# Attention bodies with the MLP as one block, maxima eight steps ahead, normalisations in halves, and the scores of a step in two pairs of heads

## The reference, cut to what matters

```
# stage 0: cross attention with a mask per batch, then MLP    (layer 0)
# stage 1: cross attention, no mask                            (layer 1)
# stage 2: self attention with one mask for all, then MLP      (layer 1)
# stage 3: causal self attention                               (layer 2)
# stage 4: cross attention, no mask, then MLP                  (layer 2)
# tail:    RMS norm, cross attention with 64-column heads      (layer 3)
q, k, v = split(norm(x) @ Wq), split(c @ Wk), split(c @ Wv)
s = einsum('bhqd,bhkd->bhqk', q, k) * scale ;  s = where(mask, -inf, s)
x = x + softmax(s) @ v @ Wo + bo
x = x + gelu(norm(x) @ W1 + b1) @ W2 + b2          # W1: 256x1024, W2: 1024x256
```

## Time and profile before

| | |
|---|---|
| median of 3 runs | 5727.45 us (5720.6 to 5732.76) |
| the profiled execution's own time | 5747.48 us |
| its span in the profile | 5745.7 us |
| PE busy | 4965.1 us (86%) |
| DVE busy | 2681.2 us (47%) |
| ACT busy | 2679.4 us (47%) |
| POOL busy | 919.7 us (16%) |
| mean granted PE clock | 0.94 of full speed |

### The profile page before, as it was taken

The page is one execution under the profiler, slowest core; times in us unless marked ns, Lnnn a source line. Parts: engine busy times, 40 slices in busy tenths (PEclk is TensorE's granted clock), DMA queues, the critical chain, the costliest instruction groups (busy, mean ns, idle before and its releaser), DMA issues.

```text
span 5745.7 us, 70587 instructions
## 1 busy us (share of the span) xinstructions
PE 4965.1 (86%) x25988; PEld 2091.8 (36%) x25988; DVE 2681.2 (47%) x5328; ACT 2679.4 (47%) x3337; POOL 919.7 (16%) x831
## 2 busy tenths in 40 slices
PE   6888888878888888888888888888876799999999
PEld 2333333332222343333443343334433333333333
DVE  4444444445556544444334446444441345555444
ACT  3555555454554554454443344565554233333333
POOL 0000010100011000011011111110010233333333
PEclk8999999988999999999998899899998899999999
DMA  1011111011111000101011111100010100000000
GB/s 52 32 34 41 47 37 41 33 53 57 52 48 54 32 29 27 37 34 37 29 50 48 53 63 58 36 32 30 32 47 23 48 12 1 11 12 12 12 12 8
DMA packets 152313, 201.93 MB, mean 35 GB/s; under 512 B 18993, under 2 KB 102321, under 8 KB 150706
## 3 DMA queue, kind: packets, MB, share of 16 engines
q1 hardware_dynamic: 151986, 197.31, 10.1%
HBM read 128.86 MB, written 68.42 MB: 34 GB/s over the span
## 4 chain that ended last, share of the span: by engine, by line
PE 65%; DVE 13%; issue 9%; ACT 6%; DMA 4%; POOL 1%; SPq 1%; DVEq 0%; POOLq 0%; ACTq 0%
PE small L555 12%; PE psT L598 7%; PE small L548 7%; PE psO L616 6%; PE small L665 6%; PE psT L767 4%; DVE nmb L986 4%; PE psS L576 4%; PE psT L602 3%; PE psT L548 2%; PE psT L732 2%; PE psO L782 2%; PE psT L555 2%; PE psT L782 2%; DVE out L983 2%
## 5 line engine op out<-in xcount | busy, mean ns | idle before, releaser
L824 ACT ACTIVATE probs<-psT 128x1024 f32<-128x1024 f32 (+3 forms) x1280 | 1158.7, 958 | 1402.9 <-PE psT L602 632.5
L986 DVE TENSOR_REDUCE nmb<-psS 128x2 bf16<-128x1024 f32 (+3 forms) x768 | 840.4, 1094 | 838.0 <-PE psS L576 535.3
L598 PE MATMUL psT<-low 32*128 32x512 f32 (+3 forms) x5120 | 781.7, 666 | 107.5 <-DVE low L1010 43.8
L983 DVE CUSTOM_DVE_ANT_0 out<-psS,pens_sb 128x512 f32<-128x512 f32 x1024 | 665.8, 688 | 135.8 <-issue 106.9
L616 PE MATMUL psO<-probs,V 128*32 128x512 f32 (+3 forms) x5120 | 684.0, 608 | 0.0
L576 PE MATMUL psS<-out 32*128 32x512 bf16 (+3 forms) x2560 | 501.6, 388 | 207.4 <-DVE nmb L986 132.0
L1128 DVE TENSOR_REDUCE parts<-psS 128x2 bf16<-128x1024 f32 x256 | 314.9, 1230 | 523.7 <-PE psS L754 523.7
L665 PE MATMUL small<-out,W 128*128 128x256 f32 x1536 | 399.6, 405 | 132.3 <-ACT out L859 38.0
L930 ACT ACTIVATE probs<-psT 128x1024 f32<-128x1024 f32 x256 | 262.0, 1023 | 526.1 <-PE psT L770 526.1
L576 PEld LDWEIGHTS psS<-out 32*128 32x128 bf16 x2560 | 123.7, 93 | 814.1 <-DVE nmb L986 326.2
L555 PE MATMUL small<-W,gel 128*128 128x256 f32 x1536 | 357.2, 386 | 16.4 <-DVE low L1010 13.5
(11 more groups left out here) (152 smaller groups left out, 5600.9 us busy)
## 6 DMA issues: line engine op xcount, KB each, us to landing
o_mid<-oT SPq DMA_DIRECT2D x160, 256.0 KB, 2.0
oN<-o_mid SPq DMA_DIRECT2D x160, 128.0 KB
oN<-r_mid SPq DMA_DIRECT2D x80, 256.0 KB
x_mid<-xe SPq DMA_DIRECT2D x40, 512.0 KB, 3.0
xw<-x_mid SPq DMA_DIRECT2D x36, 512.0 KB, 4.6
xe<-x_mid SPq DMA_DIRECT2D x36, 512.0 KB, 4.6
cT<-ctxT SPq DMA_DIRECT2D x20, 512.0 KB, 4.7
W<-wm SPq DMA_DIRECT2D x6, 1024.0 KB, 7.7
```

Of the source, the lines that this page charges most:

```text
L598: last = nc.tensor.matmul(psT[j][:, q0:S], Kf[rows_of(j), q, a, c, kt * P:(kt + 1) * P], Qf[rows_of(j), q, a, c, q0:S], start=True, stop=p ...
L824: nc.scalar.activation(probs[:, i % 2, two, q0:S], psT_all[:, two, q0:S], ACT.Exp, scale=float(DH) ** -0.5)\
L983: nc.vector.tensor_tensor_reduce(junk[:, k, :], psS[k], pens[:, 0, qt * S:(qt + 1) * S], 1.0, -3.0e38, ALU.add, ALU.max, nmb4[:, g % 2, qt ...
L986: nc.vector.tensor_reduce(nmb4[:, g % 2, qt, row:row + 33:32], psS_both[:, :, 0:n], AX, ALU.max)\
```

## The change

- LEAD is 8 in place of 6. The maxima of `cur`'s steps 8 to 15 are computed in steps 0 to 7 of its own body.
- MLP bodies: after step 9 there is one block. PE runs the 8 hidden tiles (two matmul pairs of 128x512 each) into psT banks 0 and 1 in turn, ACT takes each with one gelu of 512 columns, then PE runs the second layer in 8 parts into banks 2 and 3, DVE adds them to xe with two instructions. Between these 16 pieces PE issues the 16 max_scores of `nxt`. In the block PE also issues outputs(9). No exponential is computed in it. The eight f and four z fills are gone from `small`. In the steps 8 to 15 of an MLP body there are no max_scores.
- Other bodies: the maxima of `nxt` run in steps 8 to 15.
- PE's order of a step: max_scores 0; the scores of heads 0 and 1 with their mask, then those of heads 2 and 3 with theirs, each pair with its own wait for the exponential that frees its two banks and its own signal to ACT; even fills; max_scores 1; outputs. Where the odd slot has fills, outputs come ahead of max_scores 1, and the fills behind. The two max_scores of a step swap their pairs of heads.
- Moments and normalisations on DVE are cut in halves of two token tiles in slots of their own, and the slots of all fills are new. In a slot of DVE this work now comes ahead of the readers of fills.
- On ACT the readers of fills come ahead of the copy to oT. On POOL `scale` comes ahead of the second rsqrt of stage 0. On SP the store of group 1's oT comes ahead of the store of x, and an MLP body's x is stored when the block's sums are added.
- gel is 512 columns wide; oT, masks, cw and cn live in other buffers' space.

```diff
-LEAD = 6
+LEAD = 8
-CUR_USES = {True: {"m1": 6, "m2": 14, "m3": 20}, False: {"m1": 7, "m2": 15, "m3": 22}}
-Y_USES = {True: {"y0": 7, "y1": 8}, False: {"y0": 14, "y1": 16}}
-MLP_USES = {"h0": 11, "h1": 12, "fa0": 13, "fa1": 15, "fa2": 17, "fa3": 19, "za0": 21, "za1": 22,
-            "fb0": 23, "fb1": 25, "fb2": 26, "fb3": 27, "zb0": 29, "zb1": 30}
-CTX_USES = {True: {"c0": 8, "c1": 9}, False: {"c0": 11, "c1": 12}}
-NXT_USES = {True: {"x0": 4, "x1": 5, "q0": 9, "k0": 10, "q1": 16, "k1": 18, "v0": 24, "m0": 28, "v1": 31},
-            False: {"x0": 6, "x1": 8, "q0": 10, "k0": 12, "q1": 18, "k1": 20, "v0": 24, "v1": 26, "m0": 29}}
+MLP_AFTER = 9
+CUR_USES = {True: {"m1": 1, "m2": 15, "m3": 17}, False: {"m1": 1, "m2": 15, "m3": 21}}
+Y_USES = {True: {"y0": 10, "y1": 12}, False: {"y0": 17, "y1": 19}}
+MLP_USES = {"h0": 18, "h1": 19}
+CTX_USES = {True: {"c0": 13, "c1": 14}, False: {"c0": 12, "c1": 12}}
+NXT_USES = {True: {"x0": 7, "x1": 8, "q0": 9, "k0": 16, "q1": 21, "k1": 23, "v0": 25, "m0": 27, "v1": 29},
+            False: {"x0": 7, "x1": 9, "q0": 11, "k0": 13, "q1": 23, "m0": 25, "k1": 27, "v0": 29, "v1": 31}}
+MASKS_AT = 15
+X_STATS, X_NORMALISE = (2, 3), (5, 6)
+C_STATS, C_NORMALISE = {True: (8, 9), False: (7, 8)}, {True: (11, 12), False: (10, 11)}
+MLP_STATS, MLP_NORMALISE = (13, 14), (16, 17)
+RECIP_AT = 5
...
             def max_scores(place, u, i, k, ahead):
...
+                for e in range(2):
+                    j = 2 * (1 - k) + e
+                    last = nc.tensor.matmul(psS[e][:, 0:n], Qb[rows_of(j), q, a, c, qt * P:(qt + 1) * P], Kb[rows_of(j), q, c, 0:n],
                                             start=True, stop=u.s != CAUSAL)
...
             def exp_scores(place, u, i):
...
-                if positive(k := count("exp_done", u, 2 * i)):
-                    pe.wait_ge(sem["exp_done"], k)
-                plain = u.s not in (*MASKED, CAUSAL)
-                for j in range(4):
-                    last = nc.tensor.matmul(psT[j][:, q0:S], Kf[rows_of(j), ...], Qf[rows_of(j), ...], start=True, stop=plain)
-                for j in range(4):
-                    if u.s in MASKED: ...
-                last.then_inc(sem["st_full"], 1)
+                for pair in range(2):
+                    if positive(k := count("exp_done", u, 2 * i - 1 + pair)):
+                        pe.wait_ge(sem["exp_done"], k)
+                    for j in (2 * pair, 2 * pair + 1):
+                        last = nc.tensor.matmul(psT[j][:, q0:S], Kf[rows_of(j), ...], Qf[rows_of(j), ...], ...)
+                    for j in (2 * pair, 2 * pair + 1):
+                        if u.s in MASKED: ...
+                        if u.s == CAUSAL: ...
+                    last.then_inc(sem["st_full"], 1)
...
+            def hidden(u, m):
+                if m >= 2:
+                    pe.wait_ge(sem["f_read"], count("f_read", u, m - 1))
+                for c in range(C):
+                    last = nc.tensor.matmul(psT[m % 2], W1[:, c, m * P:(m + 1) * P], hM[:, c, :], start=c == 0, stop=c == C - 1)
+                last.then_inc(sem["f_full"], 1)
+            def from_hidden(u, t, part):
+                if t == 0 and part == 0:
+                    pe.wait_ge(sem["f_read"], count("f_read", u, FC))
+                for m in range(FC // 2 * part, FC // 2 * (part + 1)):
+                    last = nc.tensor.matmul(psT[2 + t // 2][:, (t % 2) * D:(t % 2 + 1) * D], gel[:, m, t * P:(t + 1) * P], W2[:, m, :], ...)
+                if t % 2 and part:
+                    last.then_inc(sem["z_full"], 1)
+            def mlp(place, u, cur, nxt):
+                pe.wait_ge(small_read, place.fills("prev", "h1") + 2)
+                if cur is not None:
+                    pe.wait_ge(sem["exp_done"], count("exp_done", cur, 2 * (MLP_AFTER + 1)))
+                for m in range(FC):
+                    hidden(u, m)
+                    maximum_next(m)
+                if cur is not None:
+                    outputs(cur, MLP_AFTER)
+                for t in range(T):
+                    for part in range(2):
+                        from_hidden(u, t, part)
+                        maximum_next(FC + 2 * t + part)
...
+                    if maxima:
+                        max_scores(place, u, at, 0, who == "nxt")
+                    if cur is not None:
+                        if place.body.mlp and i == MLP_AFTER + 1:
+                            pe.wait_ge(sem["z_read"], count("z_read", prev, 2))
+                        exp_scores(place, cur, i)
+                    for owner, use in place.body.at(2 * i):
+                        fill(place, owner, use, prev, cur, nxt)
+                    if maxima and not late:
+                        max_scores(place, u, at, 1, who == "nxt")
+                    if i == 0 and prev is not None:
+                        outputs(prev, STEPS - 1)
+                    if i > 0 and cur is not None and not (place.body.mlp and i == MLP_AFTER + 1):
+                        outputs(cur, i - 1)
+                    if maxima and late:
+                        max_scores(place, u, at, 1, who == "nxt")
+                    for owner, use in late:
+                        fill(place, owner, use, prev, cur, nxt)
+                    if place.body.mlp and i == MLP_AFTER:
+                        mlp(place, prev, cur, nxt)
...
+            def gelus(u):        # ACT, after slot 19 of an MLP body
+                for m in range(FC):
+                    act.wait_ge(sem["f_full"], count("f_full", u, m + 1))
+                    nc.scalar.activation(gel[:, m, :], psT[m % 2], ACT.Gelu, bias=v_(f"f{u.s}", m)).then_inc(sem["f_read"], 1)
...
+            def take_hidden(u):  # DVE, behind the block's 16 maxima
+                dve.wait_ge(sem["biased"], count("biased", u, 2))
+                for k in range(2):
+                    dve.wait_ge(sem["z_full"], count("z_full", u, k + 1))
+                    xs = xe[:, 2 * k:2 * k + 2, :]
+                    nc.vector.tensor_tensor(xs, xs, psT[2 + k].rearrange("p (t n) -> p t n", t=2), ALU.add).then_inc(sem["z_read"], 1)
```

More of the change, by code:

```diff
@@ L432, in store @@
             def store(place, u):
-                use = "zb1" if u.s in MLP else "y1"
                 dst = tokens(at_row(x_mid, u))
-                sp.wait_ge(small_read, place.fills("prev", use) + 2)
+                if u.s in MLP:
+                    sp.wait_ge(sem["z_read"], count("z_read", u, 2))
+                else:
+                    sp.wait_ge(small_read, place.fills("prev", "y1") + 2)
                 sp.dma_start(dst, xe[:]).then_inc(sem["x_out"], 16)
@@ L557, in token_major, with max_scores @@
                 return last
-            def max_scores(place, u, i, pair, ahead):
+            def max_scores(place, u, i, k, ahead):
                 g, qt = divmod(i, T)
@@ L659, in fill @@
                     last = token_major(dst, (2 * i, 2 * i + 1), oC, C, wo)
-                elif kind == "f":
-                    half, pair = "ab".index(part[0]), int(part[1])
-                    for k in range(2):
-                        m = 2 * pair + k
-                        for c in range(C):
-                            last = nc.tensor.matmul(dst[:, k * D:(k + 1) * D], W1[:, c, m * P:(m + 1) * P],
-                                                    hM[:, c, half * D:(half + 1) * D], start=c == 0, stop=c == C - 1)
-                elif kind == "z":
-                    last = token_major(dst, (int(part[1]),), gel, FC, W2)
                 else:
@@ L675, in body @@
             def body(place, prev, cur, nxt):
                 for i in range(STEPS):
-                    for half in range(2):
-                        if half == 0 and cur is not None:
-                            exp_scores(place, cur, i)
-                        if cur is not None and i + LEAD < STEPS:
-                            max_scores(place, cur, i + LEAD, half, False)
-                        if nxt is not None and i + LEAD >= STEPS:
-                            max_scores(place, nxt, i + LEAD - STEPS, half, True)
-                        if half == 0 and i == 0 and prev is not None:
-                            outputs(prev, STEPS - 1)
-                        if half == 0 and i > 0 and cur is not None:
-                            outputs(cur, i - 1)
-                        for who, use in place.body.at(2 * i + half):
-                            fill(place, who, use, prev, cur, nxt)
+                    who, u, at = ("cur", cur, i + LEAD) if i < LEAD else ("nxt", nxt, i - LEAD)
@@ new lines, in body @@
+                    maxima = u is not None and (i < LEAD or not place.body.mlp)
+                    late = place.body.at(2 * i + 1)
+                    if maxima:
[6 more added lines that the diff above has]
+                        fill(place, owner, use, prev, cur, nxt)
@@ L874, in body @@
                         exponentials(cur, i, 1)
+                    for who, use in place.body.at(slot):
```

(18 more changed lines are left out.)

175 lines of the change are left out of this document (94 added, 81 removed).

## The result

The changed kernel takes 5944.2 us (median; 5923.2 to 5954.5), the kernel before 5729.0 in the same session: ratio 1.0373, 95% interval 1.0338 to 1.0408. It is 215 us slower where 5694 us was forecast, and lies outside the range; no rival's time (5555, 5730, 5770, 5804) comes near it. The profiled execution took 5954.5 us with a span of 5952.7.

A forecast was written before the change was run, and what follows sets the result against it. It took PE to be near the bound (86% busy) but idling and slowed, with DVE's maxima setting stage 1's pace; gains and losses by body summed to -32 or -33 us, 5727.5 - 33 = 5694 us, range 5560 to 5830.

The forecast's parts named there:

- the price of the pairs: Scores split into two pairs of heads: 0.86 us more a masked step, about 0.5 a causal one, 0 without mask.
- wholly free: Side remark in the cheap-pairs rival: if pairs cost nothing in masked and causal steps, 5415 us; no row speaks for it.
- a lower clock behind a few holes: PE's clock slow after idle holes: 2.5 us in a stage 1 body, 2.5 behind the MLP block's exit.
- masked bodies longer with some 1.5 us pair to pair: Sign of being right: masked bodies longer than before, 1.5 us from a pair's first matmul to the next pair's.
- PE full in the block: Sign of being right: the MLP block takes 36 us with PE never idle.
- no wait of y0 for POOL: Sign of being right: in MLP bodies the y fill no longer waits for POOL's scale, a 5.26 us hole before.
- a hole of about 3 us behind the block: Sign of being right: at the MLP block's exit PE idles 2.8 us for DVE's last maximum and two adds.
- Cheap pairs: Rival: in masked and causal steps pairs cost half the price taken, as row groups overlap; 5555 us, chance 0.17.
- Serial pairs in unmasked steps: Rival: the second pair's wait holds PE's queue, 0.85 us a step in 16 unmasked bodies; +110, 5804 us, chance 0.18.
- Stall swap: Rival: the block's entry and exit cost what removed waits gave, stage 1 stays at DVE's pace; 5730 us, chance 0.08.
- Drains: Rival: two more tiling-mode changes cost 0.1 us each in 256 masked and 128 causal steps; 5770 us, chance 0.12.

The follow-up runs named there:

- four at once: Changed kernel with the scores of all four heads together behind one wait, then the four masks or triangles, in all stages: 5411.1 us, ratio 0.942 to the kernel before.
- the scores computed again: Changed kernel with four heads' scores together, heads 2 and 3 computed a second time between the two pairs of masks: 5785.0 us, ratio 1.0083 to the kernel before.

## Why the prediction was wrong

**The step that failed is the price of the pairs.** The prediction took 0.86 us a masked step and 0.5 a causal one, 220 + 64 = 284 us; the changed kernel pays 533. Its own side remark shows that the rest of the sum was sound as a whole: with pairs "wholly free" it gave 5415, and four at once measured 5411.1. The price is off by 249 us, and the forecast by 250. Term by term:

- Serial time, masked: 1.59 us a pair (forecast 1.5) and 1.05 a step more, inside the bounds of 0 to 1.1 but 0.19 above the value taken. 256 steps make 269 us. The two masks hold PE 0.53 as forecast; the scores of a pair 1.06 (2273.64 to 2274.70) and not the 0.96 that two heads take in the tail.
- Serial time, causal: 13.5 us a body, 0.84 a step instead of 0.5, 108 us in 128 steps. (The step of 256 columns alone is 1.70 - 0.97 = 0.73.) The forecast scaled the whole masked price by width; but the kernel before did four heads of 256 columns in 0.65 us and two cost the same, so the second group is paid in full, and the borders do not shrink with the columns.
- The clock, which the price of the pairs left out: the remaining 533 - 269 - 108, some 156 us. By bodies of the profiled executions it is 92 in the causal ones (7 x 13.1), 5 in the first of that stage, 56 in stage 0 (7 x (24.8 - 16.8)), 6 in the first of stage 2 and 4 in the others of it. The 159 us between the scores computed again and the changed kernel agree with it in sum, not body by body: over all seven, stage 0 bodies of that run are 3.4 us above four at once plus rows (147.6 against 127.4 + 16.8), those of stage 2 3.3 below (140.7 against 127.2 + 16.8). So the causal 92 are well supported; for stage 0 the clock's share may be 32 (7 x (152.2 - 147.6)) or 56. The prediction had a lower clock behind a few holes, for some 2.5 us each time. It did not reckon with waits of about 1 us behind which the clock is at half for 37.5 to 41 us, six times in seven causal bodies.

**The forecast's parts, against the kernel that has them without the pairs.** Taking the pair price out of the forecast (0.86 x 16 = 13.8 a masked body, 8 a causal one) leaves 127.8 for stage 0, 124.2 for stage 2, 85.2 for its first body and 70 for causal ones; measured with four at once 127.4, 127.2, 84.5 and 68.3. In the changed kernel stage 1 was to be 73 and is 71.2, stage 4 111 and 113.1, its first body 73 and 69.8, the last with `cur` 93 and 91.1. That the new order would pay was right, and by more than it said: 211 us on top of the rest, of which 82 in stages 1 and 3 and most of the others in MLP bodies. Stage 1's gain was laid to the order and the halves, which was right in size and half right in cause: LEAD, slots and block without them already bring that body from 82.8 to 75.0.

**The signs it named.** Right: masked bodies longer with some 1.5 us pair to pair; PE full in the block; no wait of y0 for POOL (before 107 us in 24 waits of that line, one of them); a hole of about 3 us behind the block. The block, of stage 0, its first tiles and its last maximum:

```profile
563.75 1.98 PE L678 MATMUL psT<-out,W 128*128 128x512 f32 x4 [0.94 <-ACT out L891]
565.66 0.39 PE L582 MATMUL psS<-out 32*128 32x512 bf16 x2
...
600.34 0.39 PE L582 MATMUL psS<-out 32*128 32x512 bf16 x2
```

36.6 us from the first hidden tile to the start of the last maximum, for the 36 forecast. The hole behind it is 2.84 us. None of the signs named would have caught the clock.

**The rivals.** Cheap pairs: wrong, they were dearer. Serial pairs in unmasked steps: wrong; they stand side by side (1.24 us for eight), and four at once only where masks are gives all of it. Stall swap: wrong; the block, slots and LEAD are worth 137 us. Drains: right in its direction. By the rule of the Trainium skill ("TensorEngine Tiling (Array Packing)", Key Properties) each change of mode drains the array. An estimate from the rows has the border at about 0.1 us (two masks hold PE 0.53 where two passes are 0.44), so two more borders are a fifth of a masked step's 1.05. The larger part is scores that no longer run beside each other: two groups of 1.06 in place of one of 1.17. The same section of the Trainium skill says in its second point that tiles of one mode run in parallel, and the Trainium skill's "TensorE: Matmul & The Clock Gate", Part 3, says that matmuls start and end in program order. The trace agrees with both: x8 in 1.24 when nothing stands between, x4 in 1.13 twice when a mask does, so nothing behind a full-height matmul joined the scores ahead of it. The prediction had this mechanism right for the masked steps; it did not carry it to the causal ones, nor to the clock.

**Left open.** Why the clock stays low so long with the pairs. It is low for 37.5 to 41 us behind the wait for V where the scores run on two of the four row groups at a time, for 13.7 where they run on four and then on two, for 6.8 where they run on four; but the scores computed again also add matmuls, so that run does not prove that the row groups are what counts. By the Trainium skill's "TensorE: Matmul & The Clock Gate", Part 1, the clock falls after idle time of PE, and activity brings it back. The falls of the trace do stand behind waits, short ones; but the 40.4 us of work in 41 at half the clock are not what that section leads one to expect. Block, LEAD and slots were not run apart.

## What to carry to other kernels

Matmuls on single row groups are nearly free beside each other, and only beside each other: before splitting such a group, ask what would stand between its parts, and keep full-height matmuls out of there. A second wait at the same place cost nothing; it was the interleaving that cost 533 us. Where packed matmuls lose their neighbours, price the granted clock too, even if PE hardly waits: look behind each wait of about 1 us for how long the clock stays low.

## What the runs showed of the hardware

- The granted clock was 0.77 over 664 us in which PE was 95% busy, 0.96 for the same work with four heads at once. Behind a wait of 1.40 us it was 0.50 for 41 us, with PE busy 40.4 of them; with four heads at once it was 0.50 for 6.8 us behind a wait of 1.55. A pair's scores of 256 columns took 0.70 us at the full clock and 1.22 at half.
- Two heads of 512 columns take 1.13 us and four take 1.24.
- Table loads of 1283 ns on ACT fell from 162 to 24 at the gelu and from 161 to 23 at the exponentials. No run takes their effect apart; the six MLP bodies of stage 4 are 2.1 us a body above a forecast that gave them nothing.
- A hole of 2.77 us at a block's exit was followed by a fill of 2.67 us, one of 0.53 by the same fill in 1.88. Of the 72 us that moving two additions gained, 48 are the holes; that the rest lies in the clock behind them fits these fills and is not shown for the whole.
